# A perceiver block: first batch rounded and split in the query stage, and the rounding of turned weights moved ahead of the exponential in the first half of a batch

## What is computed

```python
q_big = rope(einsum('bshk,hkq->bshq', layernorm(x) @ Wq.T, w_kc_q))
kv_r = rope(kv_c)
q_r = einsum('bshq,hqr->bhsr', q_big, W_qr)
k_r = einsum('bld,hdr->bhlr', kv_r, W_kr)
scores = einsum('bhsr,bhlr->bhsl', q_r, k_r)
attn = softmax(scores, axis=-1)
ctx_c = einsum('bhsl,bld->bhsd', attn, kv_r)
ctx_lat = einsum('bhsd,hkd->bhsk', ctx_c, w_kc_kv)
x = x + ctx_lat.reshape(B, S, H * K) @ Wo.T
```

## Time and profile before

| what | value |
|---|---|
| median of 3 runs | 1606.23 us (1604.67 to 1607.58) |
| the profiled execution | 1605.91 us |
| its span, first to last instruction | 1604.1 us |
| mean granted TensorE clock, share of full speed | 0.965 |
| busy share of the span, PE / DVE / ACT / POOL | 92% / 71% / 54% / 39% |
| query stage | to about 462 us |
| cross-attention stage | about 462 to 950 us |

### The profile page before, as it was taken

One profiled execution on the slowest core, in us unless ns is written; L12 is line 12 of the kernel. 1 busy time (PEld: TensorE's weight loads), 2 busy tenths in 40 slices (PEclk: granted clock), 3 DMA queues, 4 the chain that ended last, 5 costly groups with the idle time before them and its releaser, 6 DMA issues. The chain is left out here.

```text
span 1604.1 us, 27410 instructions
## 1 busy us (share of the span) xinstructions
PE 1471.8 (92%) x8392; PEld 1134.6 (71%) x8392; DVE 1139.9 (71%) x1952; ACT 863.3 (54%) x1859; POOL 632.8 (39%) x596
## 2 busy tenths in 40 slices
PE   4799999999967999999999867999898899999997
PEld 3577777777746888888888656888443478787876
DVE  6888788887628888888888653777687735556466
ACT  4566566656546666666666533555211355554554
POOL 4244342542036777767677513221251202222021
PEclk9899999999979999999999978999898899999999
DMA  4223334243565555555555514000244100000000
GB/s 152 70 83 107 105 110 128 71 122 88 191 197 109 129 114 118 127 111 128 111 120 120 121 20 172 1 0 0 84 173 159 43 1 1 27 0 27 0 27 27
DMA packets 141207, 140.14 MB, mean 87 GB/s; under 512 B 84438, under 2 KB 112214, under 8 KB 139996
## 3 DMA queue, kind: packets, MB, share of 16 engines
q1 hardware_dynamic: 140572, 138.60, 31.9%
q10 hardware_dynamic: 576, 0.81, 0.2%
HBM read 109.88 MB, written 27.39 MB: 86 GB/s over the span
## 5 line engine op out<-in xcount | busy, mean ns | idle before, releaser
L1031 ACT ACTIVATE c_sc_ps<-c_sc_ps,c_peak 128x257 f32<-128x257 f32 x256 | 113.6, 444 | 156.9 <-DVE c_peak L923 156.9
L77 DVE TENSOR_TENSOR b_rot_parts_low<-b_rot,b_rot_parts_high 128x1536 fp32r<-128x1536 f32 x64 | 136.5, 2132 | 20.6 <-ACT b_rot_parts_high L543 20.6
L884 POOL TENSOR_TENSOR c_mixed_low<-c_whole,c_mixed_high 128x512 fp32r<-128x512 f32 x64 | 81.9, 1280 | 131.2 <-ACT c_mixed_high L1061 131.2
L280 POOL TENSOR_TENSOR b_turned_raw<-b_turn_part 128x384 f32<-128x384 f32 x32 | 69.0, 2155 | 163.5 <-DVE b_key_parts_low L77 162.2
L1627 PE MATMUL f_ps<-f_right,f_left 128*128 128x512 f32 x256 | 116.1, 615 | 8.3 <-ACT f_raw L1670 5.9
L70 PE MATMUL c_out_ps<-c_shared_high,c_mixed_high 128*128 128x512 f32 x256 | 112.6, 440 | 8.8 <-issue 8.8
L326 DVE TENSOR_TENSOR b_rot<-b_w_qr,b_angle 128x1536 f32<-128x1536 f32 x64 | 119.5, 1867 | 0.2
L923 DVE TENSOR_REDUCE c_peak<-c_sc_ps 128x2 f32<-128x514 f32 x128 | 88.5, 691 | 42.7 <-PE c_sc_ps L72 41.6
L70 PE MATMUL b_ps<-c_shared_high,b_wq_parts_high 128*128 128x512 f32 x256 | 108.6, 424 | 6.5 <-DVE c_shared_low L77 6.5
L276 POOL TENSOR_TENSOR b_turn_part<-b_early,b_centre 128x384 f32<-128x384 f32 x64 | 84.6, 1342 | 72.9 <-DMA b_early<-early 71.3
L70 PE MATMUL e_mm_ps<-folded_high,e_h_t_high 128*128 128x512 f32 x256 | 106.4, 416 | 6.7 <-DVE e_h_t_low L77 6.6
(11 more groups left out here) (244 smaller groups left out, 4291.1 us busy)
## 6 DMA issues: line engine op xcount, KB each, us to landing
c_ends_spread<-end_weights SPq DMA_DIRECT2D x64, 256.0 KB, 3.8
carried_queries<-x SPq DMA_DIRECT2D x7, 2048.0 KB, 11.2
b_early<-early SPq DMA_DIRECT2D x15, 640.0 KB, 4.0
c_raw<-cache_t SPq DMA_DIRECT2D x64, 128.5 KB, 3.4
c_swapped<-cache_t SPq DMA_DIRECT2D x128, 64.2 KB, 3.2
f_left<-ent_in SPq DMA_DIRECT2D x16, 512.0 KB, 5.5
f_right<-ent_out SPq DMA_DIRECT2D x16, 512.0 KB, 6.9
c_q_first<-carried_queries SPq DMA_DIRECT2D x32, 224.0 KB, 3.3
```

The source lines that it names most:

```text
L77: return nc.vector.tensor_tensor(low, value, high.bitcast(F32), ALU.subtract)
L884: nc.gpsimd.tensor_tensor(mixed[1][:, w, :, u], whole[:, u % 2].rearrange("p (h s) -> p h s", h=H), mixed[0][:, w, :, u].bitcast(F32), ALU ...
L1031: last = nc.scalar.activation(sc_ps[:, 2 * v + c, 0:L], sc_ps[:, 2 * v + c, 0:L], ACT.Exp, bias=peak[:, v, c:c + 1], accum_out=total[:, v, ...
```

## The change

It does two things.

1. **Seam.** The pair of buffers for the output weights is now `Crossing.vo`, which lives on into the cross-attention stage and serves there as `q_high` and `key_high`. ACT rounds batch 0's keys and the first 14 heads of its queries in the query stage, between `store_vo` and the last two `store_qr` (`round_first`), and its last two heads after the last `store_qc` (`round_last_heads`), straight from `staged`. POOL makes the low parts behind `rotate_first`. SP's `staged_queries` has one DMA instead of two. The roundings and splits of batch 0 are gone from the start of the cross-attention stage.
2. **Even steps.** On ACT `round_turned` of an even step comes ahead of `exponential(n + 1)`, on DVE `split_turned` comes ahead of `split_kv` and `normalise(n + 1)`. Odd steps stay as they were.

The diff, cut to its core:

```diff
             crossing.rotate_first(nc, pool, spare[:, 2 * ROWS + 2 * B * G:2 * ROWS + 2 * B * G + 2 * L].rearrange("p (n l) -> p n l", n=2))
+            crossing.split_first(nc, pool)
+            crossing.split_last_heads(nc, pool, staged)
...
             repeat_to_last(act, HPAIRS, body)
+            crossing.round_first(nc, act)
             for sign in range(2):
                 store_qr(2 * HPAIRS - 1, sign)
             for sign in range(2):
                 store_qc(2 * HPAIRS - 1, 1, sign)
+            act.wait_ge(qc_stored, 8 * HPAIRS)
+            crossing.round_last_heads(nc, act, staged)
...
     def staged_queries(self, sp, staged):
-        for u in range(2):
-            sp.dma_start(self.q[:, u, (H - 2) * S:].bitcast(F32), staged[:, u].rearrange("p h s -> p (h s)")).then_inc(self.q_loaded[u], 16)
+        sp.dma_start(self.q[:, 1, (H - 2) * S:].bitcast(F32), staged[:, 1].rearrange("p h s -> p (h s)")).then_inc(self.q_loaded[1], 16)
+
+    def round_first(self, nc, act):
+
+        n = (H - 2) * S
+        act.wait_ge(self.w_vo_out[0], 32 * H // 2)
+        act.wait_ge(self.rotated, 1)
+        nc.scalar.activation(self.key_high[0], self.keys[:], ACT.Copy).then_inc(self.key_rounded, 1)
+        act.wait_ge(self.q_loaded[0], 16)
+        nc.scalar.activation(self.q_high[:, 0, 0:n], self.q[:, 0, 0:n].bitcast(F32), ACT.Copy).then_inc(self.q_rounded, 1)
...
             nc.gpsimd.memset(kv_later[:, :, L:], 0.0).then_inc(crossing.padded, 1)
-            split_keys(0, 0)
-            split_queries(0, 0)
             pool.wait_ge(crossing.padded, 2)
...
                     if half == 0:
+                        split_turned(n, u, half)
                         split_kv(b, u)
                     if half == 1 and (u or known(i, 1)):
                         add_end(i - (u == 0), (u - 1) % BT)
                     if more:
                         normalise(n + 1, 1 - half)
-                    split_turned(n, u, half)
+                    if half == 1:
+                        split_turned(n, u, half)
...
                     b = BT * i + u
+                    if half == 0:
+                        round_turned(n, b, u, half)
                     if not (isinstance(n, int) and n == PAIRS - 1):
                         exponential(n + 1, 1 - half)
-                    round_turned(n, b, u, half)
+                    if half == 1:
+                        round_turned(n, b, u, half)
...
             nc.scalar.activation(scratch[:, 0:1], ident[:, 0:1], ACT.Exp).then_inc(warmed, 1)
-            round_keys(0, 0)
-            round_queries(0, 0, 0)
             exponential(0, 0)
```

More of the change, by code:

```diff
@@ L123, in query_path @@
         qr_sb = spare[:, 2 * ROWS:2 * ROWS + 2 * B * G].rearrange("p (n b s) -> p n b s", n=2, b=B)
-        w_vo = pair("b_w_vo", [P, 2, D])
+        w_vo = crossing.vo
         ps = ctx.enter_context(nc.psum_tensor("b_ps", [P, 8, D], F32))
@@ L698, in __init__ @@
         self.pool_chained, self.rotated, self.padded = sem("c_pool_chained"), sem("c_rotated"), sem("c_padded")
+        self.q_rounded, self.q_split, self.key_rounded, self.key_split = (sem(f"c_{n}") for n in ("q_rounded", "q_split", "key_rounded", "key_split"))
+        self.vo = [ctx.enter_context(nc.sbuf_tensor(f"c_vo_{part}", [P, 2, D], F32R)) for part in ("high", "low")]
+        self.q_high = self.vo[0]
+        self.key_high = [self.vo[1][:, u, 0:L + 1] for u in range(2)]
+        self.first_key_low = ctx.enter_context(nc.sbuf_tensor("c_first_key_low", [P, L + 1], F32R))
         self.table_loaded = sem("c_table_loaded")
@@ L720, in staged_queries, with split_first, round_last_heads, split_last_heads @@
     def staged_queries(self, sp, staged):
-        for u in range(2):
-            sp.dma_start(self.q[:, u, (H - 2) * S:].bitcast(F32), staged[:, u].rearrange("p h s -> p (h s)")).then_inc(self.q_loaded[u], 16)
+        sp.dma_start(self.q[:, 1, (H - 2) * S:].bitcast(F32), staged[:, 1].rearrange("p h s -> p (h s)")).then_inc(self.q_loaded[1], 16)
[6 more added lines that the diff above has]
+        nc.scalar.activation(self.q_high[:, 0, 0:n], self.q[:, 0, 0:n].bitcast(F32), ACT.Copy).then_inc(self.q_rounded, 1)
+    def split_first(self, nc, pool):
+        n = (H - 2) * S
+        pool.wait_ge(self.key_rounded, 1)
+        nc.gpsimd.tensor_tensor(self.first_key_low[:], self.keys[:], self.key_high[0].bitcast(F32), ALU.subtract).then_inc(self.key_split, 1)
+        pool.wait_ge(self.q_rounded, 1)
+        nc.gpsimd.tensor_tensor(self.q[:, 0, 0:n], self.q[:, 0, 0:n].bitcast(F32), self.q_high[:, 0, 0:n].bitcast(F32), ALU.subtract).then_inc(self.q_split, 1)
+    def round_last_heads(self, nc, act, staged):
+        nc.scalar.activation(self.q_high[:, 0, (H - 2) * S:], staged[:, 0].rearrange("p h s -> p (h s)"), ACT.Copy).then_inc(self.q_rounded, 1)
+    def split_last_heads(self, nc, pool, staged):
+        pool.wait_ge(self.q_rounded, 2)
+        nc.gpsimd.tensor_tensor(self.q[:, 0, (H - 2) * S:], staged[:, 0].rearrange("p h s -> p (h s)"), self.q_high[:, 0, (H - 2) * S:].bitcast(F32),
+                                ALU.subtract).then_inc(self.q_split, 1)
     W_VO_GROUPS = [0, H // 2, H - 2, H]
@@ L770, in cross_attention @@
         q = [crossing.q[:, u] for u in range(2)] + [q_later[:, u] for u in range(BT - 2)]
-        q_high = sb("c_q_high", [P, 2, H * S], F32R)
-        keys = pair("c_key", [P, 2, LE])
+        q_high, key_high = crossing.q_high, crossing.key_high
+        later_key_low = sb("c_later_key_low", [P, LE], F32R)
+        key_low = [crossing.first_key_low[:], later_key_low[:]]
         peak = sb("c_peak", [P, 2, 2])
@@ L791, in cross_attention @@
         q_loaded, rotated_, pool_chained = crossing.q_loaded, crossing.rotated, crossing.pool_chained
-        q_rounded, q_split, key_rounded, key_split = (sem(f"c_{n}") for n in ("q_rounded", "q_split", "key_rounded", "key_split"))
+        q_rounded, q_split, key_rounded, key_split = crossing.q_rounded, crossing.q_split, crossing.key_rounded, crossing.key_split
         kv_turned, kv_rounded, kv_split = (sem(f"c_{n}") for n in ("kv_turned", "kv_rounded", "kv_split"))
@@ L808, in queries_in @@
         def queries_in(u, t):
-            return 32 * (t + 1)
+            return 32 * (t + 1) if u else 32 * t + 16
         def in_tiles(engine, tile):
@@ L887, in split_queries @@
             def split_queries(b, u):
-                pool.wait_ge(q_rounded, b + 1)
+                pool.wait_ge(q_rounded, b + 2)
                 nc.gpsimd.tensor_tensor(q[u], q[u].bitcast(F32), q_high[:, u % 2].bitcast(F32), ALU.subtract).then_inc(q_split, 1)
@@ L892, in split_keys @@
                 pool.wait_ge(key_rounded, b + 1)
-                nc.gpsimd.tensor_tensor(keys[1][:, u % 2], kv_even[u], keys[0][:, u % 2].bitcast(F32), ALU.subtract).then_inc(key_split, 1)
+                nc.gpsimd.tensor_tensor(key_low[u % 2], kv_even[u], key_high[u % 2].bitcast(F32), ALU.subtract).then_inc(key_split, 1)
             nc.gpsimd.memset(kv_later[:, :, L:], 0.0).then_inc(crossing.padded, 1)
-            split_keys(0, 0)
-            split_queries(0, 0)
             pool.wait_ge(crossing.padded, 2)
@@ L1054, in round_keys @@
                 wait(act, scored, 2 * b - 2)
-                nc.scalar.activation(keys[0][:, u % 2], kv_even[u], ACT.Copy).then_inc(key_rounded, 1)
+                nc.scalar.activation(key_high[u % 2], kv_even[u], ACT.Copy).then_inc(key_rounded, 1)
             def round_mixed(b, u, t, w):
@@ L1110, in score @@
                 if half == 0:
-                    pe.wait_ge(q_split, b + 1)
+                    pe.wait_ge(q_split, b + 2)
                     pe.wait_ge(key_split, b + 1)
@@ L1116, in score @@
                     at = slice((2 * half + c) * P, (2 * half + c + 1) * P)
-                    last = multiply_parts(nc, sc_ps[:, 2 * half + c, 0:LE], [q_high[:, u % 2, at], q[u][:, at]], [a[:, u % 2] for a in keys], True, True)
+                    last = multiply_parts(nc, sc_ps[:, 2 * half + c, 0:LE], [q_high[:, u % 2, at], q[u][:, at]], [key_high[u % 2], key_low[u % 2]], True, True)
                 last.then_inc(scored, 1)
```

## The result

The changed kernel takes **1590.15 us** in the median of 5 runs (1587.88 to 1593.08), the kernel before 1606.23 (1604.67 to 1607.58). The ratio is 0.9901, interval 0.9887 to 0.9914: 15.9 us less, with 2.2 us of uncertainty each way. Forecast were 1594.0, in a range of 1588.5 to 1600.5.

What follows compares the result with a forecast made beforehand. PE was taken to bound the cross-attention tiles, waiting there for DVE's low part of the turned weights. -4.85 - 8.2 + 0.8 = -12.25 us from the profiled 1605.91 gave 1593.7, as a median 1594.0, range 1588.5 to 1600.5.

Steps and rivals of the forecast that it cites:

- Term 1: Start of cross-attention: without batch 0's roundings and splits on the path, the first score comes 4.85 us earlier.
- The rival in which the seam gives nothing: POOL's queue or batch 1's query DMA holds `score(2)` where it was; only 0.59 us gained there, 1598.2 us; chance 0.07.
- Term 2: Regular tiles: even distances become about 3.29 us, odd ones mostly 3.62; 0.62 us less per tile, 8.2 us in all.
- The rival in which the even steps give nothing: Regular tiles: the later exponential takes what the earlier low part gives; only the seam gains, 1602.2 us; chance 0.10.
- Term 3: Tile 0, even steps before the projections: the exponential behind the rounding costs 0.1 to 0.3 us a batch, +0.8 us.
- The clock: Start of cross-attention: low clock taken as unchanged, back at full 15 us after the first score; counted as 0.
- the rival in which the clock stays at full: Over the seam PE's shorter idleness keeps the clock from falling; another 2.1 us gained, 1591.9 us; chance 0.17.
- The slower rival: Even steps: late turns delay exponentials on in-order ACT; loses once even distances pass about 3.57 us; 1617.5 us; chance 0.05.

Runs made afterwards that it cites:

- e6_warm: Kernel before, with 32 unread identity products keeping PE at work over the change of stage (16 before it, 16 ahead of the first score); 1604.61 us, ratio 0.9993.
- e1_seam_only: Kernel before with the change's seam alone, even steps of ACT and DVE as before; 1596.63 us, ratio 0.9941.
- e2_even_only: Kernel before with the even steps' new order on ACT and DVE alone, old seam; 1596.23 us, ratio 0.9946.
- e7_kv_first: Changed kernel with DVE's low part of the turned keys back ahead of the weights' low part in even steps; 1591.00 us, ratio 0.9918.
- e5_ends_first: Changed kernel with SP storing and spreading the last tile's first two batches' end weights before the rotation wait and five loads; 1580.86 us, ratio 0.9839.
- e3_act_half: Changed kernel with DVE's half undone: ACT rounds first, DVE's low part stays last in even steps; 1615.29 us, ratio 1.0064.

## Why the prediction was right, and where it missed

- **Term 1, the seam (-4.85).** Right. In the trace of the whole change -5.12 at the first score, -5.37 at the first turn, -5.27 at `score(2)`; the blocks change 0.99 us earlier against the last ACT row (4.38 to 3.39 us), where I had 0.59. Both vary with the execution: the three profiles with the old seam have the first turn 12.20 to 13.12 us behind the last ACT row (12.20 is `e6_warm`) and the change of blocks 3.71 to 4.38 us behind it, the seven with the new seam 7.75 to 8.32 and 3.22 to 3.74. The 4.85 fits that. Each successor that I followed behaved: `store_qr` stands 5.83 us ahead of that row in both kernels, the table load is hidden, and `score(2)` keeps a wait for POOL but moves along. The rival in which the seam gives nothing is refuted by `e1_seam_only`. That run gained 9.5 us, at least 7.2 by its interval: more than this term. What the excess is, the clock or something else, stays open.
- **Term 2, regular even steps (-8.2).** Right, and the pattern too: 3.25 for 3.29, then 3.62. The regular tile gained 0.74 where I had 0.62 (0.67 in `e2_even_only`). Over 13 tiles it is 7.58, since tiles 3 to 6 took 28.2 to 28.4 us and not 28.0. Some small waits of `add_end` there name the spread of the end weights (0.9 us in all from 520 to 710, as much as in the kernel before); the rest of that excess I can't place. The rival in which the even steps give nothing is refuted by `e2_even_only`. The 3.29 that I took for what PE needs holds for the old seam (3.27 to 3.30 in `e2_even_only`); in the changed kernel it is 3.24 to 3.28, and 3.25 to 3.28 in `e1_seam_only`. Why is not known; it is 0.1 us a tile.
- **Term 3, tile 0 (+0.8).** The direction is in the trace, the place is not: in tile 0 the even distances stay at 3.17 to 3.20, and it is the odd ones that became 3.27 where they were 3.18. That is 0.1 a batch, 0.4 a tile (25.80 us against 25.51 in `e1_seam_only`). Tile 1 got no longer. About 0.4 too much.
- **The clock (0).** This is the term that was mis-sized. I took the low stretch as unchanged because PE is poorly filled behind the seam. Between the two profiles it shrank from 20 to 7 us, and tile 0 became 1.75 us shorter where term 3 alone makes it 0.3 longer, so about 2.1. That is the price I gave for the rival in which the clock stays at full, though the clock did fall, twice. As a gain of the change it is not shown: `e2_even_only` and `e7_kv_first` have low stretches of other lengths with the same seams, and the median of `e6_warm` does not resolve it. What is left is a gain by the clock of 0 to 3 us.
- **The sum.** Between the two profiled executions the terms with rows give -5.37 at the seam, -7.58 in the 13 tiles and +0.3 in tile 0: -12.6, where I had -12.25. Tile 0's clock, -2.1, and four stretches that I had at nothing (+1.52, -0.77, +0.80, -2.61, in all -1.1) make the rest of the -15.76. So these terms came out for the reasons given; that they agree to 0.4 us is in part luck, since terms 1 and 3 fell better than forecast and term 2 worse, by about half a us each. The median, 1590.15, is 3.8 us below the forecast of 1594.0, with 2.2 us of uncertainty; that part I can't assign.
- **The slower rival.** Its mechanism is real and close by: with ScalarE's half of the edit alone, even distances are 3.81 to 3.90 and the kernel is slower by 0.64%. The point from which it decides, 3.57, was passed there, and not in the change.
- **Not seen.** The stall of 10 us at batch 60 was in the trace of before. It did not bear on the forecast, because it is in both kernels, but it was worth as much as either part of the change.

## What to carry to other kernels

When two engines pass work on in order, look in the starved engine's queue for an instruction whose inputs are ready before the one it idles for, and move it into that idle time; then check that the engine that feeds it pays less than this. Here the feeding engine's half alone made the kernel slower (`e3_act_half`), and both halves together made it faster. At the end of a loop, look at what the queue of DMA issues does between the last iteration and the drain: one wait for something else there held up every engine for 10 us.

## What was not expected of the hardware

- In the changed kernel the granted clock was low from 463.0 to 466.5, back at full within 4 us of the first score, with PE then idle for a moment, and fell again from 469.5 to 473.5. In the profile of the kernel before it stayed low for 20 us over the same work.
- The 10 us stall brings a low clock behind it. In the changed kernel the clock was at 0.62 from 905 to 912 us, the end of the stall, and at 0.58 in the 6 us behind it, where PE was busy all the time; in `e5_ends_first` it was 1.00 from 880 to 924 us. The last tile became 12.6 us shorter there, but the whole run only 9.3, so a cost of the stall beyond its length is not shown.
- Two profiled executions of kernels with the same order of work in a stretch differ there by up to 1.5 us (tile 1: 28.96 and 27.46), so a single profile carries no term that small. Here the granted clock goes with it. Tile 1 took 28.96 in the kernel before and 27.54 in `e6_warm`, which has the same order there, and 28.19 in the changed kernel against 27.11 in `e5_ends_first`; in the longer one of each pair the clock fell for a few us within the tile (504 to 510 and 500 to 504), in the shorter one it did not.
